# ScalarE copies the mask into the scores banks, and all engines in a new order

## What is computed

```python
# once:  x = x + tanh(g_xattn) * cross_attention(layernorm(x), ctx)
def attn_layer(x, Wqkv, qs, ksc, Wo):              # HEADS, DIM_HEAD, WINDOW = 16, 64, 32
    q, k, v = split(x @ Wqkv)                      # 16 heads of 64
    q, k = l2norm(q) * qs, l2norm(k) * ksc
    q = q * cos * scale + rotate_half(q) * sin * scale
    k = k * cos / scale + rotate_half(k) * sin / scale
    out = local_attention(q, k, v)
    return out @ Wo

def local_attention(q, k, v):                      # each window of 32 sees itself and the one before
    sim = einsum('bhwie,bhwje->bhwij', bq, bk2) * QK_SCALE
    sim = where(mask, -finfo.max, sim)
    attn = softmax(sim, -1)
    return einsum('bhwij,bhwje->bhwie', attn, bv2)

def ffn_layer(x, g, bln, W1, b1, W2, b2):
    xn = (x - mean) / sqrt(var + 1e-05) * g + bln
    a, gate = split(xn @ W1 + b1)
    return a * gelu(gate) @ W2 + b2
# six times:  x = x + attn_layer(x);  x = x + ffn_layer(x);  at last  x1 + tanh(g_ffn) * x
```

## Time and profile before

| | |
|---|---|
| median of 3 runs | 1567.43 us (1566.67 to 1567.67) |
| the profiled execution | 1565.26 us, its span 1563.4 us |
| busy: PE, PEld | 1499.3 us (96%), 1251.6 us (80%) |
| busy: DVE, ACT, POOL | 1317.1 (84%), 1167.1 (75%), 1180.8 (76%) |
| granted TensorE clock, mean | 0.983 |
| chain that ended last | PE 92% |

### The profile page before, as it was taken

The page is one execution under the profiler, slowest core; times in us unless marked ns, Lnnn a source line. Parts: engine busy times, 40 slices in busy tenths (PEclk is TensorE's granted clock), DMA queues, the critical chain, the costliest instruction groups (busy, mean ns, idle before and its releaser), DMA issues.

```text
span 1563.4 us, 80230 instructions
## 1 busy us (share of the span) xinstructions
PE 1499.3 (96%) x31136; PEld 1251.6 (80%) x31136; DVE 1317.1 (84%) x2497; ACT 1167.1 (75%) x2333; POOL 1180.8 (76%) x1166
## 2 busy tenths in 40 slices
PE   4489999999999999999999999999999999999997
PEld 3367888888888888888888888888888888888886
DVE  3578889888888988988888898888889889889883
ACT  3457788788778778877877887887787787777774
POOL 1277877878887887788788878888878877877781
PEclk8789999999999999999999999999999999999998
DMA  5111111011111111101012110112111012010101
GB/s 147 43 43 32 29 37 43 26 50 55 36 30 32 43 40 59 42 27 36 26 43 62 36 42 26 36 32 72 30 32 30 20 31 64 23 30 20 30 25 34
DMA packets 41462, 62.40 MB, mean 40 GB/s; under 512 B 3662, under 2 KB 30412, under 8 KB 41420
## 3 DMA queue, kind: packets, MB, share of 16 engines
q1 hardware_dynamic: 41420, 61.84, 13.5%
HBM read 18.84 MB, written 1.05 MB: 13 GB/s over the span
## 4 chain that ended last, share of the span: by engine, by line
PE 92%; issue 1%; ACT 1%; DVE 0%; POOL 0%; ACTq 0%; DVEq 0%; POOLq 0%
PE bank L1035 16%; PE bank L1105 12%; PE bank L1117 11%; PE bank L1028 10%; PE bank L1029 9%; PE bank L1030 8%; PE bank L1078 8%; PE bank L1152 5%; PE bank L1141 3%; PE bank L1060 3%; PE bank L1142 2%; PE bank L1143 2%; PE bank L1131 1%; PE bank L1125 1%; PE bank L1014 0%
## 5 line engine op out<-in xcount | busy, mean ns | idle before, releaser
L406 POOL TENSOR_TENSOR u<-u,t 128x512 f32<-128x512 f32 x384 | 490.4, 1282 | 23.8 <-DVE t L821 23.8
L420 POOL TENSOR_TENSOR u<-u,rn 128x512 f32<-128x512 f32 x384 | 392.7, 1044 | 75.8 <-ACT rn L572 75.8
L426 POOL TENSOR_TENSOR P<-P,rs 128x512 f32<-128x512 f32 x192 | 196.3, 1043 | 123.6 <-DVE rs L845 123.6
L821 DVE TENSOR_TENSOR t<-bank,TS 128x512 f32<-128x512 f32 x384 | 258.3, 683 | 28.4 <-ACT sq L561 25.8
L1028 PE MATMUL bank<-Wl,xsh 128*128 (+1 forms) x576 | 273.6, 475 | 5.8 <-POOL xsl L400 3.0
L812 DVE TENSOR_TENSOR u<-bank,TC 128x512 f32<-128x512 f32 x384 | 262.1, 683 | 10.1 <-issue 6.5
L805 DVE TENSOR_REDUCE ss<-sq 128x8 f32<-128x512 f32 x384 | 250.5, 673 | 2.9 <-ACT sq L561 2.9
L1029 PE MATMUL bank<-Wh,xsl 128*128 (+1 forms) x576 | 228.4, 397 | 0.0
L1030 PE MATMUL bank<-Wh,xsh 128*128 (+1 forms) x576 | 227.9, 396 | 0.0
L561 ACT ACTIVATE sq<-bank 128x512 f32<-128x512 f32 x384 | 221.5, 605 | 6.2 <-PE bank L1030 5.7
L1035 PE MATMUL bank<-shape_constants,u 128*128 128x128 f32 x1536 | 219.0, 275 | 3.3 <-POOL u L420 3.2
(11 more groups left out here) (102 smaller groups left out, 2960.4 us busy)
## 6 DMA issues: line engine op xcount, KB each, us to landing
vs<-v SPq DMA_DIRECT2D x96, 384.0 KB, 3.3
Wraw<-in_L_ffn_Wqkv_dram SPq DMA_DIRECT2D x72, 117.5 KB, 2.1
WoS<-in_L_ffn_Wo_dram SPq DMA_DIRECT2D x6, 512.0 KB, 3.7
W1h<-Wh SPq DMA_DIRECT2D x6, 341.0 KB, 2.5
W1l<-Wl SPq DMA_DIRECT2D x6, 341.0 KB, 2.9
Wraw<-in_L_ffn_W_dram SPq DMA_DIRECT2D x12, 116.0 KB, 2.2
OT<-in_x_dram SPq DMA_DIRECT2D x2, 512.0 KB, 5.7
v<-in_ctx_dram SPq DMA_DIRECT2D x2, 512.0 KB, 7.0
```

What stands on the lines that cost most here:

```text
L406: nc.gpsimd.tensor_tensor(u[:, r, c], u[:, r, c], t2[:, r, c % 2], ALU.add).then_inc(add_done[c], 1)
L420: nc.gpsimd.tensor_tensor(by_head(u[:, r, c]), by_head(u[:, r, c]), spread(rn[:, r, HC * c:HC * c + HC], HC, DH), ALU.mult).then_inc(qk_re ...
L821: nc.vector.tensor_tensor(halves(t2[:, r, c % 2]), halves(bank_of("chunk", c, r)[:])[:, :, ::-1, :], TS[:, layer(it - lag), c % 2].broadca ...
```

## The change

**The mask.** `identb`, `maskb` and the product on PE go. ACT's new `masks` copies the fp32 mask, broadcast four times, from SBUF into the scores bank (128 x 512), once that bank's last readers are done, and counts `seeded[e]`. `scores` waits for both `seeded` and for q and k. Whole-array transposes of q, k and P stay as they were.

**Names and buffers.** `qT` and `kT` become one tensor `qkT`; `queries` and `keys` become `heads_out(k)`, one 128 x 512 copy each as before. `row_sums` loses its reciprocal; `reciprocals` makes one for both halves (128 x 16), so two per pair stand where there were four, and `divide` of either half waits for it.

**The order.** All four compute engines get a new order and the banks new users. In words: `project_out`, `centre` and `variance` move from the turn after a pair's chunks to the second turn after, as do `turn_p` and `values` of r = 1; `v_chunk(0)` of r = 1 moves to the start of the next turn; `x_parts` now waits only for that one, and `x_rest` moves within POOL's turn to a place behind `bound_norms(1,1)`. On SP `shifted_values` of both r now follow one another, one turn after the pair's chunks. In the cross attention POOL makes the tables before the copies of the context, and ACT does its four `upper_part` in a row behind the copies `pT4`, where before two of them stood ahead of the copies `xhT4`.

```diff
-        qT = sb("qT", [128, 2, 4, 128])
-        kT = sb("kT", [128, 2, 4, 128])
+        qkT = sb("qkT", [128, 2, 2, 4, 128])
...
-        x_read = (ch_full[2], v_full[0])
+        x_read = (v_full[0], v_full[0])
...
         BANK_USERS = [
-            [("chunk", 1, 0, 0), ("up", 0, 0, 2), ("v", 1, 0, 0), ("chunk", 1, 1, 0)],
...
+            [("scores", 0, 0, 1), ("turn_qk", 0, 1, 1), ("chunk", 2, 0, 0), ("chunk", 1, 1, 0), ("chunk", 0, 1, 0)]]
...
-                def queries(s, lag, r):
...
+                def masks(e, lag, r):
+                    n = (it - lag) * 2 + r
+                    for readers, value in bank_left(it - lag, "scores", e, r):
+                        act.wait_ge(readers, value)
+                    nc.scalar.copy(bank_of("scores", e, r)[:].rearrange("p (t n) -> p t n", t=4),
+                                   maskf[:].unsqueeze(1).broadcast_to([128, 4, 128])).then_inc(seeded[e], 1)
+
+                def heads_out(k, lag, r):
+                    n = (it - lag) * 2 + r
+                    s, w = divmod(k, 2)
+                    act.wait_ge(qkT_full[k], n_(n) + 1)
+                    act.wait_ge(sc_full[s], n_((it - lag - HEADS_BACK[k][r]) * 2 + 1 - r) + 1)
+                    nc.scalar.copy(qkT[:, s, w].rearrange("p t n -> p (t n)"),
+                                   bank_of("turn_qk", k, r)[:]).then_inc(qk_out[k], 1)
...
                     nc.vector.tensor_reduce(psum[:, r, e], P[:, r, e], AX, ALU.add).then_inc(sum_done[e], 1)
-                    dve.wait_ge(sum_done[e], n_(n) + 1)
-                    nc.vector.reciprocal(rs[:, r, e], psum[:, r, e]).then_inc(rs_done[e], 1)
+
+                def reciprocals(lag, r):
+                    n = (it - lag) * 2 + r
+                    dve.wait_ge(sum_done[0], n_(n) + 1)
+                    dve.wait_ge(sum_done[1], n_(n) + 1)
+                    nc.vector.reciprocal(rs[:, r].rearrange("p e g -> p (e g)"),
+                                         psum[:, r].rearrange("p e g -> p (e g)")).then_inc(rs_done, 1)
...
-                def masks(e, lag, r):
-                    freed("scores", e, r)
-                    nc.tensor.matmul(bank_of("scores", e, r)[:].rearrange("p (t n) -> p t n", t=4), identb[:],
-                                     maskb[:].unsqueeze(1).broadcast_to([128, 4, 128]),
-                                     start=True, stop=False, skip_group_check=True)
-
                 def scores(s, lag, r):
                     n = (it - lag) * 2 + r
-                    pe.wait_ge(q_ready[s], n_(n) + 1)
-                    pe.wait_ge(k_ready[s], n_(n) + 1)
+                    pe.wait_ge(seeded[0], n_(n) + 1)
+                    pe.wait_ge(seeded[1], n_(n) + 1)
+                    pe.wait_ge(qk_out[2 * s], n_(n) + 1)
+                    pe.wait_ge(qk_out[2 * s + 1], n_(n) + 1)
```

447 lines of the change are left out of this document (222 added, 225 removed).

## The result

The changed kernel takes 1549.3 us (median of 4 runs, 1546.4 to 1551.6) beside 1567.1 for the kernel before on the same chip: a ratio of 0.989, 95% interval 0.987 to 0.991. It is faster, by 18 us. The forecast was 52, and its range ended at 1546: the time lies outside, by 3 us. The profiled execution took 1550.4 us, its span is 1548.4.

The account below looks back on a forecast made before the run. PE's list of work bounds each turn. Terms of -48 (turns), -8 (start), -5 (second turn) and +9 (end) give -52 against 1565.3, or 1513; forecast median 1515 us, own range 1502 to 1530 (turns 28.9 to 29.5), whole range 1494 to 1546.

Parts of the forecast that it names:

- The masks leave PE: Per turn: four mask matmuls leave PE at 0.22 us a slot, -0.87 us; ACT's copies lie beside PE's work.
- The wait of a chunk for v: Per turn: the next chunk no longer waits for ACT's copy of v; -0.23 us (0 to -0.3).
- One spell of small tiles less: Per turn: three entries to small tiles where there were four; -0.10 us (0 to -0.20), about 0 if the seam drains.
- Three tight places: Variance to scores of r = 1, turn start, chunk 2 to chunk 1: +0.15 us together (0 to +0.8).
- the first: Tight place from the variance over ACT to the scores of r = 1: late by 0.2 us or less.
- Start: Before the first scores: ACT's copies no longer stand behind weight pieces that wait for DMA; -8 us (-10 to -3).
- Second turn: It lacks all lag 2 work, so POOL sets it: about 24.5 us in place of 29.8, -5 (-7 to 0).
- The 46 turns: Between first and last scores of r = 0: each turn falls by 1.05 us to 29.17, -48 us over 46 turns.
- End: Lag 2 work comes back behind the last pair, after its scores of r = 0: +9 us (+4 to +12).
- The fourth: Rival: the masks' slots come back as a wait for `seeded`, through late banks or long copies; 1555 us, chance 0.08.
- the second: Rival: the tight places bind, all three late by 0.2 to 0.3, and the seam drains; 1542 us, chance 0.16.
- The slower case: Rival: the reciprocal for both halves delays POOL's divides and `x_rest`, so PE's first chunk waits; 1575 us, chance 0.10.

Follow-up runs that it names:

- run 7: The changed kernel with PE writing the masks again, without ACT's mask copies and the waits for them; the new order stays: 1578.4 us, 1.008.
- run 12: The changed kernel with each of ACT's four mask copies of a turn cut to 8 of every 128 columns: 1545.9 us, 0.988.
- run 1: The changed kernel without the two waits for the seeded banks in the second score call of a pair half: 1544.1 us, 0.987.
- runs 8, 9: The first: changed kernel with fewer PE waits beside spells of small tiles, 1531.3 us, 0.979; the second: also without those another wait covers, 1527.5 us, 0.975.
- run 2: The changed kernel with a turn's first chunk product moved between the scores of r = 0 and the values of r = 1: 1592.0 us, 1.017.
- run 5: The changed kernel with two turns written out ahead of the loop in place of three: 1547.4 us, 0.988.
- run 11: The changed kernel with 128 further semaphore increments at the start of PE's list: 1565.4 us, 0.999.

## Why the prediction was right in its main mechanism and wrong in its time

- **The masks leave PE.** Right: 0.22 a slot in run 7, copies of 618 ns, hidden (run 12). The scores' wait for them, which I counted at nothing, cost 0.22 a turn as issue time, of which run 1 got back 0.11.
- **The wait of a chunk for v.** Right: it is gone, and the one wait for a partner that PE's starts show in the middle is another, that of `up` for `xfl`.
- **One spell of small tiles less.** Entering is 0.10, and the seam is free of it (runs 8, 9), but five waits stood in the seam, so it cost 0.35 where 0.15 was to be had. The rule that I weighed there, the Trainium skill's (TensorEngine Tiling (Array Packing), Key Properties), that a change of tiling mode drains the array, isn't what the 0.35 was: with other waits and the same tiles 0.146 are left. Whether a drain is part of these 0.146 no run here shows.
- **Three tight places.** None of the three bound as I had placed them; the +0.15 stood for the wrong thing. A fourth bound, which hangs on the variance as the first does: `up` behind `xfl`, 0.07 a turn. And in place of the +0.15 stood some 0.57 of issue time at four spots (0.22 + 0.20 + 0.15). This step failed: I counted waits only by when they are met. Together that is 0.49 more than allowed for, where the turn missed by 0.35; the other terms must have given some 0.14 more than forecast, and which of them isn't resolved. The turn of 29.52 lies just past the forecast's own 29.5.
- **Start.** Right: 91.4 against 92.1.
- **Second turn.** I had POOL set it and priced PE's work at full clock. The two are busy alike, 23.56 and 23.58 of 28.0 us, so that POOL sets it isn't shown. The clock of 0.88 is about the size of the miss.
- **The 46 turns are not equal.** The costliest miss: I took third, fourth and switch turn as steady ones, though the trace of before had the third at 31.7 and the fourth at 30.9, and I averaged these into 30.22. Nor did I ask what "issue" in the middle of a call means. This step failed too: PE stops for its own code where that runs for the first time, and the clock falls behind some of the stops. Misses of 12.0 and 1.8 us.
- **End.** The work came back behind the last pair, as foretold; stops and half clock in the last pair's turn make 6.5 of the 8.1 us between 52.5 and 60.6.
- **Rivals.** The fourth, 1555, and the second, 1542, came nearest by their numbers, 6 and 7 us off. The fourth's mechanism is not what happened: of the 0.88 of the four slots 0.22 went to the waits for `seeded`, as issue time and not because the copies were late. The second's remark on the four waits of `scores` was the right trail, but of its late results there is only the 0.07 at `up`. The slower case did not come: POOL's `x_rest` ended 1.65 to 1.8 us ahead of need, where I had placed it 1.7, yet with no reserve behind the scores (run 2).

## What to carry to other kernels

Where small-tile matmuls stand in a row, PE is bound by its queue: count each instruction that only waits (one holds two waits) or computes a register as about 0.1 us at the end of such a spell or inside it, met or not, and take out what another wait covers. What is saved so can come back as a wait for a partner that PE now reaches too early; a busy share of 100% doesn't show that, but a constant distance from a partner's end to PE's start over many turns does. Look at the turns one by one before averaging them: those whose code runs for the first time have another price, and it changes with every edit that moves the code. Differences of a few us between two versions may be nothing else.

## What was not expected of the hardware

- PE's code comes in packets of 16,384 bytes, and a stop ends 2.2 to 2.9 us after the packet has begun; with 1.3 us for 256 instructions PE can be faster than that.
- Behind stops of 2.15 and 1.51 us (start to start) in the third turn, of 2.06 in the fourth and of 1.79 at the end the granted clock was 0.50 to 0.57 over 3.3 to 6.5 us. Behind the one of 1.52 at the switch of loops, behind two of 1.6 and 1.5 in the third turn of run 12, and behind those of 0.75 to 1.38 in the kernel before, it stayed at 1.00: the length of the stop alone doesn't tell.
- An unchanged turn costs 29.6 or 33.3 us, by whether its code has run before (run 5).
- 128 semaphore increments on PE, with nothing else to do, took 19.5 us, 0.15 each (run 11).
